# A half-precision-split transformer layer on one core: where two halves of an attention sum are joined, and how mean and variance are finished

## The chip, the cores and the metric

The kernel runs on one core of a Trainium2 chip. The metric is the time of one execution on the device in microseconds (us). The core has a matrix engine (TensorE, "PE" in the profile, its weight loads "PEld"), a vector engine (VectorE, "DVE"), an activation engine (ScalarE, "ACT"), a general engine (GpSimd, "POOL") and a queue engine that here only issues transfers (SyncE, "SP"). Each engine works through its own list of instructions in order; between engines the program orders work by semaphores.

## The reference

One pre-norm transformer layer over 8192 tokens (4 sequences of 2048) of width 256:

```python
x = x + attn(_layernorm(x), Wq, Wk, Wv, Wo)      # 16 heads of 16, causal, window 64
x = x + ffn(_layernorm(x), W1, b1, W2, b2)       # W1, W2 rounded to -1, 0, 1; relu; 1024 wide

def _layernorm(x, axis=-1, eps=1e-05):
    m = jnp.mean(x, axis=axis, keepdims=True)
    v = jnp.var(x, axis=axis, keepdims=True)
    return (x - m) / jnp.sqrt(v + eps)
```

Both norms need, for each token, the negative mean and the variance plus 1e-5. The attention output of a token is the sum over at most 64 keys of softmax weight times value.

## The kernel before

The tokens are cut into 16 chunks of 512. The whole program is written as one loop over slots n (16 slots belong to a chunk, about 2.5 us each in the steady part), and every engine walks the same slots with a list of what it does in each. Work of three chunks is in flight at a time: stage A (norm, Q, K and V of the next chunk), the attention of the present one (16 steps n, four for each group g of four heads), and stage C (output projection, second norm and feed-forward of the chunk before). The slot of each piece is fixed by the tables at the head of the file. A value is carried as a high and a low half-precision part, so many results are written twice, first by ACT (high), then by DVE (low).

In each slot n the attention goes through all engines: PE writes the scores into a PSUM bank (`scores`, L924); DVE takes the negative maximum (`negm`, L671); ACT takes the exponential and its sums (`p`, L457, four pairs of instructions); DVE takes the reciprocal of the sums (`rden`, L678); POOL multiplies (`p`, L358); DVE transposes 32 by 32 blocks (`pt`, L684); ACT (L466) or POOL (L376) makes the high part `th`, and POOL the low part `tl` (L382). On DVE the order within a slot is: `rden`, `pt`, `o_add` where there is one, `negm`, then the work of stages C and A, the statistics last.

Two places are touched by the change.

**Joining the two halves of the attention sum.** After each group g of a chunk PE has left 128 x 512 sums in the PSUM bank `pvbank` (L944): partitions 0 to 63 hold one half of each sum and 64 to 127 the other. In `o_copy` (slot 9 of the group's four) ACT copies partitions 0 to 63 into the SBUF tile `ohalf`. In `o_add` DVE adds partitions 64 to 127 to it and writes `osum`, at partitions 64 * (g % 2) on, so groups 0 and 2 go to partition 0 and groups 1 and 3 to partition 64. From the second chunk on DVE first waits until `osum` of the chunk before has been read (semaphores `s_olo0` and `s_olo1`, which POOL and DVE raise). PE's next sums wait for `s_osum`. Of a chunk's 16 slots DVE has `o_add` in slots 9 (group 0), 13 (group 1), 1 (group 2) and 5 (group 3).

**Finishing the statistics.** For stage A (`a_aggr`, once a chunk, 128 x 4 values) and stage C (`c_stats`, twice a chunk, 128 x 2 values) DVE runs its statistics instructions, then two small instructions: one writes the negative mean (`meanA`, `meanC`), the other the variance plus 1e-5 (`veA`, `veC`). Both are tensor_reduce here: the negated maximum over one element, and the sum over two, the variance and a constant 1e-5 that lies beside it in the third column of `mvA` and `mvC`. POOL then takes the power -1/2 (`rstdA`, `rstdC`) and the shift, and ACT applies them (`xnA`, `xnC`). Of a chunk's 16 slots, the two `c_stats` stand in slots 8 and 14 and `a_aggr` in slot 10.

Of the kernel before, what the change touches and what calls it, by code (L numbers as in the profile page):

```python
# [5 lines left out]
CH = 512  # L6
# [43 lines left out]
def stage_a(n, pos):  # L50
    return chunk_at(n, pos, 1)
# [4 lines left out]
def norm_at(n, pos):  # L56
    c, late = stage_a(n, pos), stage_a(n - 7, pos)
    return late if late in (1, 2) else None if c in (1, 2) else c
# [8 lines left out]
def stage_c(n, pos):  # L67
    return chunk_at(n, pos, -1)

def group_at(n, lag):
    g, r = divmod(n - lag, 4)
    return g if r == 0 and 0 <= g < 4 * NCH else None
# [3 lines left out]
def values_at(n, lag):  # L77
    return 0 if n == lag + 2 else group_at(n, lag) or None
# [34 lines left out]
def build(nc, x_d, wq_d, wk_d, wv_d, wo_d, w1_d, b1_d, w2_d, b2_d, identf_d, mask_d, maskf_d, out_d):  # L113
    f32, f16, b16 = mybir.dt.float32, mybir.dt.float16, mybir.dt.bfloat16
    ALU, ACT, AX = mybir.AluOpType, mybir.ActivationFunctionType, mybir.AxisListType
# [4 lines left out]
    with ExitStack() as ctx:  # L120
        def sb(name, shape, dt):
            return ctx.enter_context(nc.sbuf_tensor(name, shape, dt))

        def sem(name):
            return ctx.enter_context(nc.semaphore(name))
# [20 lines left out]
        xTC = [sb(f"xTC{p}", [128, 2, 256], f16) for p in "hl"]  # L146
        stA = sb("stA", [128, 4, 6], f32)
        stC = sb("stC", [128, 2, 6], f32)

        mvA = sb("mvA", [128, 4, 3], f32)  # L150
        mvC = sb("mvC", [128, 2, 3], f32)
        veA = sb("veA", [128, 4], f32)
        veC = sb("veC", [128, 2], f32)
        meanA = sb("meanA", [128, 4], f32)
        meanC = sb("meanC", [128, 2], f32)
# [15 lines left out]
        th = [sb(f"th{i}", [128, 1600], f16) for i in range(2)]  # L171
        tl = [sb(f"tl{i}", [128, 1600], f16) for i in range(2)]
        osum = sb("osum", [128, 2, CH], f32)
        ohalf = sb("ohalf", [64, CH], f32)
        oT = [sb(f"oT{p}", [128, 2, CH], f16) for p in "hl"]
        hT = [sb(f"hT{p}", [128, 8, CH // 2], f16) for p in "hl"]
        bt = sb("bt", [128, F + D], f32)
# [6 lines left out]
        sbank, pvbank, cbank = banks[0:3], banks[3], banks[6:8]  # L184
# [14 lines left out]
        s_alo, s_cdv, s_osum, s_olo1 = sem("s_alo"), sem("s_cdv"), sem("s_osum"), sem("s_olo1")  # L199
        s_stA, s_agA, s_mvA, s_xnA = sem("s_stA"), sem("s_agA"), sem("s_mvA"), sem("s_xnA")  # L200
        s_stC, s_agC, s_mvC, s_xnC = sem("s_stC"), sem("s_agC"), sem("s_mvC"), sem("s_xnC")
# [6 lines left out]
        s_oc, s_ohi, s_whi, s_abs, s_mask = sem("s_oc"), sem("s_ohi"), sem("s_whi"), sem("s_abs"), sem("s_mask")  # L208
# [3 lines left out]
        s_car, s_oh0, s_olo0, s_hp = sem("s_car"), sem("s_oh0"), sem("s_olo0"), sem("s_hp")  # L212
# [206 lines left out]
        def _(e):  # L419
# [101 lines left out]
                             a_bank(c, w)[:, :].rearrange("p (a b) -> p a b", b=64), ACT.Copy, scale=1 / WS).then_inc(s_ahi, 1)  # L521

            def o_copy(gg):
                e.wait_ge(s_pv, gg + 1)
                e.activation(ohalf[:, :], pvbank[0:64, :], ACT.Copy).then_inc(s_oc, 1)

            def c_t(c, h):
                e.wait_ge(s_c, USE[c, f"t{h}"] + 1)
# [8 lines left out]
            for n in SLOTS:  # L537
# [23 lines left out]
                c = stage_c(n, X_DMA)  # L561
# [5 lines left out]
                gg = values_at(n, PV_LAG + 1)  # L567
                if gg is not None:
                    o_copy(gg)
                for h in range(2):  # L570
                    c = stage_c(n, C_T[h] + 1)
                    if c is not None:
                        c_t(c, h)
                    for f in range(4):
                        c = stage_c(n, C_F[h] + f + 1)
                        if c is not None:
                            c_f(c, h, f)
                for t in range(2):
                    c = stage_a(n, A_T[t] + 1)
                    if c is not None:  # L580
                        a_t(c, t)
                    c = stage_a(n, A_Q[t] + 1)
                    if c is not None:
                        a_q(c, t)
                    c = stage_a(n, A_K[t] + 1)
                    if c is not None:
                        a_k(c, t)
                    c = stage_a(n, A_V[t] + 1)
# [4 lines left out]
                for u in range(2):  # L593
                    c = stage_c(n, C_NORM[u])
                    if c is not None:
                        c_norm(c, u)
                    c = norm_at(n, A_NORM[u])
                    if c is not None and (c, u) != (0, 1):
                        a_norm(c, u)
                gg = group_at(n, O_SPLIT1)  # L600
# [4 lines left out]
        def _(e):  # L605
            def consts():
                e.memset(mhalf[:, :], -0.5).then_inc(s_const, 1)
                e.memset(mvA[:, :, 2:3], 1e-5)
                e.memset(onesf[:, :], 1.0)
                e.memset(ones[:, :], 1.0).then_inc(s_const, 1)  # L610
                e.memset(mvC[:, :, 2:3], 1e-5)

# [86 lines left out]
            def a_aggr(c):  # L701
                e.wait_ge(s_stA, 4 * c + 4)
                if c >= 1:
                    e.wait_ge(s_rsA, c)
                for t in range(4):
                    ins = e.bn_aggr(mvA[:, t, 0:2], stA[:, t, :])
                ins.then_inc(s_agA, 1)
                e.wait_ge(s_agA, c + 1)
                e.tensor_reduce(meanA[:, :], mvA[:, :, 0:1], AX.X, ALU.max, negate=True)
                e.tensor_reduce(veA[:, :], mvA[:, :, 1:3], AX.X, ALU.add).then_inc(s_mvA, 1)  # L710

            def a_t(c, k):
                w = 8 * c + k
# [22 lines left out]
                                       scalar=1 / WS, in1=hi, op0=ALU.mult, op1=ALU.subtract).then_inc(s_alo, 1)  # L736

            def o_add(gg):
                c, g = gg // 4, gg % 4
                e.wait_ge(s_oc, gg + 1)  # L740
                if c >= 1:
                    e.wait_ge((s_olo0, s_olo1)[g // 2], c)
                e.tensor_tensor(osum[64 * (g % 2):64 * (g % 2) + 64, g // 2, :], pvbank[64:128, :], ohalf[:, :],
                                ALU.add).then_inc(s_osum, 1)

            def o_low(c):
                e.wait_ge(s_ohi, c + 1)
# [8 lines left out]
            def c_stats(c, u):  # L756
                h = 2 * c + u
                e.wait_ge(s_cdv, USE[c, f"wo{u}"] + 1)
                for t in range(2):
                    e.bn_stats(stC[:, t, :], xs[c % NX][:, 2 * u + t, :]).then_inc(s_stC, 1)  # L760
                e.wait_ge(s_stC, 2 * h + 2)
                if h >= 1:
                    e.wait_ge(s_rsC, h)
                for t in range(2):
                    ins = e.bn_aggr(mvC[:, t, 0:2], stC[:, t, :])
                ins.then_inc(s_agC, 1)
                e.wait_ge(s_agC, h + 1)
                e.tensor_reduce(meanC[:, :], mvC[:, :, 0:1], AX.X, ALU.max, negate=True)
                e.tensor_reduce(veC[:, :], mvC[:, :, 1:3], AX.X, ALU.add).then_inc(s_mvC, 1)

            def c_t(c, h):
                e.wait_ge(s_chi, SPLIT[c, f"t{h}"] + 1)
# [10 lines left out]
            for n in SLOTS:  # L783
                if n == SLOTS[0]:
                    consts()
# [17 lines left out]
                gg = values_at(n, O_ADD)  # L803
                if gg is not None:
                    o_add(gg)
                if 0 <= n - L_MAX < NQ:
                    biggest(n - L_MAX)
                for u in range(2):
                    c = stage_c(n, C_WO[u] + 1)
                    if c is not None:  # L810
                        residual(c, u, f"wo{u}")
                    c = stage_c(n, C_T[u] + 1)
                    if c is not None:
                        c_t(c, u)
                    for f in range(4):
                        c = stage_c(n, C_F[u] + f + 1)
                        if c is not None:
                            c_f(c, u, f)
                    c = stage_c(n, C_Y[u] + 2)
                    if c is not None:  # L820
                        residual(c, u, f"y{u}")
                for t in range(2):
                    c = stage_a(n, A_T[t] + 1)
                    if c is not None:
                        a_t(c, t)
                    c = stage_a(n, A_Q[t] + 1)
                    if c is not None:
                        a_q(c, t)
                    c = stage_a(n, A_K[t] + 1)
                    if c is not None:  # L830
                        a_k(c, t)
                    c = stage_a(n, A_V[t] + 1)
# [4 lines left out]
                for u in range(2):  # L837
                    c = norm_at(n, A_STATS[u])
                    if c is not None:
                        a_stats(c, u)  # L840
                        if u:
                            a_aggr(c)
                    c = stage_c(n, C_STATS[u])
                    if c is not None:
                        c_stats(c, u)
                gg = group_at(n, O_SPLIT1)
# [294 lines left out]
```

## Time and profile before

| | |
|---|---|
| runs | 710.91, 713.70, 713.49 us; median 713.49 us |
| the profiled execution | 710.91 us, its span 709.1 us |
| mean granted clock of TensorE, as a share of full speed | 0.986 |
| busy share of the span | PE 93%, ACT 90%, DVE 88%, POOL 84% |
| one chunk in the steady part | 40.0 us, from 98.85 us to about 618.85 us, 13 times |
| DVE busy in such a chunk | 37.1 to 37.8 us |

"Busy" counts the time in which at least one instruction of the engine runs. An instruction's start as recorded usually lies 0.07 to 0.09 us ahead of the recorded end of the one before it on DVE, since the engine takes it in while the last one drains; so what an instruction costs its engine is the distance from its start to the next start, not its own duration. The chain of work that ended last, which part 4 of the page sums up, is followed back from the last instruction: at each step to what released it. The steady part repeats itself to within a few hundredths of a us from chunk to chunk, so one chunk (338.85 to 378.85 us) stands for the others.

### The profile page before, as it was taken

What the parts mean: (1) busy time and instruction counts of PE and PEld (TensorE: products, weight loads), DVE (VectorE), ACT (ScalarE), POOL (GpSimd) and SP (SyncE); (2) the same over time, 40 slices, a digit from 0 to 9 for tenths busy, and PEclk for the clock granted to TensorE, in tenths of its full rate; (3) what the DMA queues carried; (4) which work ended last, traced back from release to release, by engine and by line L of the source; (5) the groups of instructions that cost most, each with busy time, mean ns of one, the idle gap of its engine ahead of it and who ended that gap; (6) DMA issues with size and microseconds to landing.
All of it is one profiled execution on the core that took longest, in us unless ns stands there. A gap on an engine that the chain in (4) does not pass through costs nothing.

```text
span 709.1 us, 24653 instructions
## 1 busy us (share of the span) xinstructions
PE 662.0 (93%) x8168; PEld 564.2 (80%) x8168; DVE 627.4 (88%) x1596; ACT 636.1 (90%) x2680; POOL 597.6 (84%) x836
## 2 busy tenths in 40 slices
PE   7649779999999999999999999999999999998796
PEld 4437568888888888888888888888888888887685
DVE  5697888999999899999999899999999899898764
ACT  3778989999999999999999999999999999998832
POOL 8277999898989989898989989898989989889820
PEclk9979999999999999999999999999999999999999
DMA  8575436365554636455464637465554536352000
GB/s 294 101 103 79 64 55 74 75 83 96 69 99 80 85 68 96 79 73 108 70 95 86 86 69 97 74 78 106 72 90 65 81 69 75 73 60 47 17 31 31
DMA packets 430773, 57.65 MB, mean 81 GB/s; under 512 B 403380, under 2 KB 422198, under 8 KB 430648
## 3 DMA queue, kind: packets, MB, share of 16 engines
q1 hardware_dynamic: 419784, 46.97, 44.9%
q10 hardware_dynamic: 10864, 9.11, 4.6%
q8 instruction: 66, 1.08, 0.7%
q14 instruction: 59, 0.48, 0.2%
HBM read 12.00 MB, written 8.39 MB: 29 GB/s over the span
## 4 chain that ended last, share of the span: by engine, by line
ACT 32%; PE 28%; POOL 17%; issue 14%; DVE 7%; DMA 1%; ACTq 1%; SPq 0%; POOLq 0%; DVEq 0%
ACT p L457 15%; POOL p L358 7%; PE ps L1034 6%; POOL tl L382 6%; PE ps L981 5%; ACT xnC L484 4%; PE ps L944 4%; ACT xnA L474 3%; PE ps L1007 3%; PE ps L924 3%; PE ps L992 3%; POOL th L376 2%; DVE negm L671 2%; ACT hTh L534 2%; PE ps L1046 2%
## 5 line engine op out<-in xcount | busy, mean ns | idle before, releaser
L457 ACT ACTIVATE p<-ps,negm 128x96 f32<-128x96 f32 x1024 | 341.4, 379 | 13.7 <-DVE negm L671 13.6
L382 POOL TENSOR_TENSOR tl<-pt,th 128x384 f16<-128x384 f32 x256 | 235.3, 919 | 50.6 <-ACT th L466 39.0
L457 ACT ACTIVATION_READ_ACCUMULATOR p<-ps,negm 128x1 f32 x1024 | 252.2, 247 | 0.0
L358 POOL TENSOR_TENSOR p<-p,rden 128x384 f32<-128x384 f32 x256 | 211.9, 828 | 12.9 <-DVE rden L678 11.5
L684 DVE STREAM_TRANSPOSE pt<-p 128x384 f32<-128x384 f32 x256 | 141.7, 554 | 11.5 <-POOL p L358 9.9
L671 DVE TENSOR_REDUCE negm<-ps 128x4 f32<-128x384 f32 x256 | 135.6, 530 | 6.7 <-PE ps L924 4.5
L924 PE MATMUL ps<-k,qbd 128*128 128x96 f16 x2048 | 130.0, 207 | 0.0
L924 PEld LDWEIGHTS ps<-k,qbd 128*128 128x128 f16 x2048 | 116.5, 99 | 13.5 <-issue 0.5
L944 PE MATMUL ps<-th,vb 128*128 128x96 f16 (+1 forms) x1120 | 97.9, 203 | 10.5 <-POOL tl L382 5.3
L944 PEld LDWEIGHTS ps<-th,vb 128*128 128x128 f16 x1120 | 92.6, 98 | 13.3 <-POOL tl L382 8.6
L1034 PE MATMUL ps<-xTCh,w1T 128*128 128x256 f16 x512 | 97.6, 272 | 0.0
L944 PE MATMUL ps<-tl,vb 128*128 128x96 f16 (+1 forms) x1120 | 97.3, 203 | 0.0
L944 PEld LDWEIGHTS ps<-tl,vb 128*128 128x128 f16 x1120 | 92.2, 98 | 0.0
L534 ACT ACTIVATE hTh<-ps 128x512 f16<-128x512 f32 x128 | 79.9, 624 | 13.2 <-PE ps L1034 13.0
L780 DVE SCALAR_TENSOR_TENSOR hTl<-ps,hTh 128x512 f16<-128x512 f32 x128 | 86.4, 677 | 4.7 <-ACT hTh L534 4.7
L376 POOL CAST th<-pt 128x384 f16<-128x384 f32 x144 | 72.4, 503 | 0.8 <-PE ps L944 0.8
L1034 PE MATMUL ps<-xTCl,w1L 128*128 128x256 f16 x256 | 69.8, 273 | 0.0
L1034 PE MATMUL ps<-xTCl,w1T 128*128 128x256 f16 x256 | 69.7, 272 | 0.0
L919 PE MATMUL ps<-mask,identb 128*128 128x256 bf16 x240 | 65.9, 275 | 3.1 <-ACT p L457 3.1
L466 ACT ACTIVATE th<-pt 128x384 f16<-128x384 f32 x112 | 64.3, 574 | 3.3 <-DVE pt L684 3.2
L1046 PE MATMUL ps<-w2T,hTl 128*128 128x256 f16 x512 | 66.5, 273 | 0.5 <-DVE hTl L780 0.5
L1046 PE MATMUL ps<-w2T,hTh 128*128 128x256 f16 x512 | 66.4, 273 | 0.0
(136 smaller groups left out, 1406.3 us busy)
## 6 DMA issues: line engine op xcount, KB each, us to landing
k<-kst SPq DMA_DIRECT2D x62, 288.0 KB, 4.1
vb<-vd SPq DMA_DIRECT2D x256, 32.0 KB, 2.6
out<-x SPq DMA_DIRECT2D x32, 256.0 KB, 2.4
qbd<-qs SPq DMA_DIRECT2D x252, 32.0 KB, 2.4
x<-in_L_attn_hidden ACTq DMA_DIRECT2D x15, 512.0 KB, 5.1
vb<-in_L_ffn_W SPq DMA_DIRECT2D x2, 1024.0 KB, 8.4
k<-kst ACTq DMA_DIRECT2D x2, 288.0 KB, 3.7
x<-in_L_attn_hidden SPq DMA_DIRECT2D x1, 256.0 KB, 3.2
```

The source lines that it names most:

```text
L358: e.tensor_tensor(p3, p3, rden[n % 4][:, :].unsqueeze(2).to_broadcast([128, 4, 96]), ALU.mult).then_inc(s_nm, 1)
L376: e.tensor_copy(th[g % 2][:, o], pt[n % 3][:, :]).then_inc(s_hp, 1)
L382: e.tensor_tensor(tl[g % 2][:, o], pt[n % 3][:, :], th[g % 2][:, o], ALU.subtract).then_inc(s_lo, 1)
L457: ins = e.activation(p[:, 96 * u:96 * u + 96], bank[:, 96 * u:96 * u + 96], ACT.Exp, bias=m[:, u:u + 1], accum_out=r[:, u:u + 1])
L534: e.activation(hT[0][:, 2 * f:2 * f + 2, :].rearrange("p a b -> p (a b)"), c_bank(c, f"f{h}{f}")[:, :], ACT.Relu).then_inc(s_chi, 1)
L671: e.tensor_reduce(negm[n % 4][:, :], sbank[n % 3][:, 0:384].rearrange("p (a b) -> p a b", b=96), AX.X, ALU.max, negate=True).then_inc(s_mx, 1)
L684: e.transpose(pt[n % 3][:, :], pr[n % NP][:, :]).then_inc(s_tr, 1)
L780: e.scalar_tensor_tensor(out=lo, in0=c_bank(c, f"f{h}{f}")[:, :], scalar=0.0, in1=hi, op0=ALU.max, op1=ALU.subtract).then_inc(s_cdv, 1)
L924: ins = e.matmul(bank[:, 96 * u:96 * u + 96], qbd[g // 2][:, g % 2, 128 * blk:128 * blk + 128], ks[g][:, m, 32 * blk:32 * blk + 96], start ...
L944: ins = e.matmul(pvbank[:, 32 * i0:32 * i1], lhs, rhs, start=(k == k0 and tt is th), stop=(k == 15), skip_group_check=True)
L1034: ins = e.matmul(bank[:, o], w, xTC[xp][:, k, :], start=(xp + k == 0), stop=(xp + k == 2))
L1046: ins = e.matmul(bank[:, o], hT[hp][:, f, t * 128:(t + 1) * 128], w2T[:, f, :], start=False, stop=(f == 7 and hp == 1))
```

## The change

In the statistics the two tensor_reduce of each pair become tensor_scalar, with immediate scalars: the mean times -1, the variance plus 1e-5. The constant column and its two memsets go. Nothing is moved to another place.

In the joining of the sums ACT now copies partitions 64 to 127 of `pvbank` straight into `osum`, at the partitions where the result belongs, and DVE adds partitions 0 to 63 of `pvbank` to it in place. The tile `ohalf` goes. The wait for `s_olo0` or `s_olo1` goes from DVE's `o_add` to ACT's `o_copy`.

```diff
@@ ACT
             def o_copy(gg):
+                c, g = gg // 4, gg % 4
                 e.wait_ge(s_pv, gg + 1)
-                e.activation(ohalf[:, :], pvbank[0:64, :], ACT.Copy).then_inc(s_oc, 1)
+                if c >= 1:
+                    e.wait_ge((s_olo0, s_olo1)[g // 2], c)
+                e.activation(osum[64 * (g % 2):64 * (g % 2) + 64, g // 2, :], pvbank[64:128, :],
+                             ACT.Copy).then_inc(s_oc, 1)
@@ DVE, consts
-                e.memset(mvA[:, :, 2:3], 1e-5)
...
-                e.memset(mvC[:, :, 2:3], 1e-5)
@@ DVE, a_aggr
-                    ins = e.bn_aggr(mvA[:, t, 0:2], stA[:, t, :])
+                    ins = e.bn_aggr(mvA[:, t, :], stA[:, t, :])
...
-                e.tensor_reduce(meanA[:, :], mvA[:, :, 0:1], AX.X, ALU.max, negate=True)
-                e.tensor_reduce(veA[:, :], mvA[:, :, 1:3], AX.X, ALU.add).then_inc(s_mvA, 1)
+                e.tensor_scalar(meanA[:, :], mvA[:, :, 0], -1.0, None, ALU.mult)
+                e.tensor_scalar(veA[:, :], mvA[:, :, 1], 1e-5, None, ALU.add).then_inc(s_mvA, 1)
@@ DVE, o_add
-                c, g = gg // 4, gg % 4
+                g = gg % 4
+                dst = osum[64 * (g % 2):64 * (g % 2) + 64, g // 2, :]
                 e.wait_ge(s_oc, gg + 1)
-                if c >= 1:
-                    e.wait_ge((s_olo0, s_olo1)[g // 2], c)
-                e.tensor_tensor(osum[64 * (g % 2):64 * (g % 2) + 64, g // 2, :], pvbank[64:128, :], ohalf[:, :],
-                                ALU.add).then_inc(s_osum, 1)
+                e.tensor_tensor(dst, pvbank[0:64, :], dst, ALU.add).then_inc(s_osum, 1)
@@ DVE, c_stats
-                e.tensor_reduce(meanC[:, :], mvC[:, :, 0:1], AX.X, ALU.max, negate=True)
-                e.tensor_reduce(veC[:, :], mvC[:, :, 1:3], AX.X, ALU.add).then_inc(s_mvC, 1)
+                e.tensor_scalar(meanC[:, :], mvC[:, :, 0], -1.0, None, ALU.mult)
+                e.tensor_scalar(veC[:, :], mvC[:, :, 1], 1e-5, None, ALU.add).then_inc(s_mvC, 1)
```

DVE's list at the end of slot 8 and the start of slot 9 of a chunk, before: the pair of the statistics, what stands right behind it, and the first `o_add` of the chunk. The names ahead of the arrow are what is written, those behind it what is read (`ps` is a PSUM bank).

```order
L765 BN_AGGR mvC<-stC 128x2 [waits s_rsC,s_stC]
L765 BN_AGGR mvC<-stC 128x2
L768 TENSOR_REDUCE meanC<-mvC 128x2 [waits s_agC]
L769 TENSOR_REDUCE veC<-mvC 128x2
L678 RECIPROCAL rden<-rsum 128x4 [waits s_nm,s_ex]
L684 STREAM_TRANSPOSE pt<-p 128x384 [waits s_lo,s_nm]
L743 TENSOR_TENSOR osum<-ps,ohalf 64x512 [waits s_olo0,s_oc]
L671 TENSOR_REDUCE negm<-ps 128x4 [waits s_ex,s_sc]
```

The same place in the changed kernel:

```order
L763 BN_AGGR mvC<-stC 128x2 [waits s_rsC,s_stC]
L763 BN_AGGR mvC<-stC 128x2
L766 TENSOR_SCALAR meanC<-mvC 128x2 [waits s_agC]
L767 TENSOR_SCALAR veC<-mvC 128x2
L678 RECIPROCAL rden<-rsum 128x4 [waits s_nm,s_ex]
L684 STREAM_TRANSPOSE pt<-p 128x384 [waits s_lo,s_nm]
L742 TENSOR_TENSOR osum<-ps,osum 64x512 [waits s_oc]
L671 TENSOR_REDUCE negm<-ps 128x4 [waits s_ex,s_sc]
```

Every instruction stands where it stood; two have another operation, and `o_add` has one wait less and reads its own output tile.

## Rows read from the trace of the kernel before

**Rows 1.** The page: busy time and share; shares of the chain that ended last.
```profile
PE 662.0 (93%) x8168; PEld 564.2 (80%) x8168; DVE 627.4 (88%) x1596; ACT 636.1 (90%) x2680; POOL 597.6 (84%) x836
...
ACT 32%; PE 28%; POOL 17%; issue 14%; DVE 7%; DMA 1%; ACTq 1%; SPq 0%; POOLq 0%; DVEq 0%
```

**Rows 2.** Windows: length, busy PE, PEld, DVE, ACT, POOL, clock, DMA share, GB/s.
```profile
338.85:378.85 40.00, 39.77 (x505) 34.24 (x504) 37.61 (x98) 38.76 (x167) 36.15 (x52) 1.00 0.55 85
```

**Rows 3.** The chain in order of time, one chunk: start, time on the chain, what.
```profile
373.72 0.04 DVE meanC L768
...
373.79 0.06 DVE veC L769
...
375.25 0.57 DVE negm L671
...
377.12 1.10 ACT xnC L484 x2
...
378.26 0.66 PE ps L1019 x4
```

**Rows 4.** Timeline, slot 8 into 9: start, duration, engine, line, operation, [idle before].
```profile
373.07 0.91 POOL L382 TENSOR_TENSOR tl<-pt,th 128x384 f16<-128x384 f32 x1
...
373.72 0.15 DVE L768 TENSOR_REDUCE meanC<-mvC 128x2 f32<-128x2 f32 x1
...
373.94 0.55 DVE L684 STREAM_TRANSPOSE pt<-p 128x384 f32<-128x384 f32 x1
374.11 0.83 POOL L358 TENSOR_TENSOR p<-p,rden 128x384 f32<-128x384 f32 x1
...
374.52 0.69 DVE L743 TENSOR_TENSOR osum<-ps,ohalf 64x512 f32<-64x512 f32 x1
...
375.25 0.56 DVE L671 TENSOR_REDUCE negm<-ps 128x4 f32<-128x384 f32 x1
...
375.72 0.74 DVE L699 BATCH_NORM_STATS2 stA<-x 128x6 f32<-128x256 f32 x2
...
375.84 0.34 ACT L457 ACTIVATE p<-ps,negm 128x96 f32<-128x96 f32 x1 [0.75 <-DVE negm L671]
```

**Rows 5.** Timeline near 39 us, in the weights' preparation: DVE and POOL.
```profile
39.08 0.92 POOL L382 TENSOR_TENSOR tl<-pt,th 128x384 f16<-128x384 f32 x1
...
39.24 0.78 DVE L648 TENSOR_SCALAR nthr<-thr 128x2 f32<-128x2 f32 x1
...
39.96 0.83 POOL L358 TENSOR_TENSOR p<-p,rden 128x384 f32<-128x384 f32 x1
```

**Rows 6.** Timeline near 644 us: a DVE operation that reads two SBUF tiles.
```profile
643.91 0.92 POOL L382 TENSOR_TENSOR tl<-pt,th 128x384 f16<-128x384 f32 x1
...
644.79 1.28 POOL L358 TENSOR_TENSOR p<-p,rden 128x384 f32<-128x384 f32 x1
...
644.16 1.22 DVE L748 TENSOR_TENSOR oTl<-osum,oTh 128x512 f16<-128x512 f32 x1
```

**Rows 7.** Timeline, slot 14: the second pair of stage C and what follows.
```profile
347.60 0.51 POOL L376 CAST th<-pt 128x384 f16<-128x384 f32 x1
...
348.08 0.15 DVE L768 TENSOR_REDUCE meanC<-mvC 128x2 f32<-128x2 f32 x1
...
348.19 0.91 POOL L382 TENSOR_TENSOR tl<-pt,th 128x384 f16<-128x384 f32 x1
...
350.40 0.33 ACT L457 ACTIVATE p<-ps,negm 128x96 f32<-128x96 f32 x1
```

**Rows 8.** Timeline, slot 10: the pair of stage A.
```profile
378.55 0.16 DVE L709 TENSOR_REDUCE meanA<-mvA 128x4 f32<-128x4 f32 x1
...
378.70 0.91 POOL L382 TENSOR_TENSOR tl<-pt,th 128x384 f16<-128x384 f32 x1 [1.19 <-ACT th L466]
```

**Rows 9.** Timeline of ACT, slot 5: the copy of a group's sums and its follower.
```profile
362.93 0.66 ACT L525 ACTIVATE ohalf<-ps 64x512 f32<-64x512 f32 x1
363.40 0.67 ACT L534 ACTIVATE hTh<-ps 128x512 f16<-128x512 f32 x1
```

More of the change, by code:

```diff
@@ L148, in build @@
         stC = sb("stC", [128, 2, 6], f32)
-        mvA = sb("mvA", [128, 4, 3], f32)
-        mvC = sb("mvC", [128, 2, 3], f32)
+        mvA = sb("mvA", [128, 4, 2], f32)
+        mvC = sb("mvC", [128, 2, 2], f32)
         veA = sb("veA", [128, 4], f32)
@@ L173, in build @@
         osum = sb("osum", [128, 2, CH], f32)
-        ohalf = sb("ohalf", [64, CH], f32)
         oT = [sb(f"oT{p}", [128, 2, CH], f16) for p in "hl"]
@@ L764, in c_stats @@
                 for t in range(2):
-                    ins = e.bn_aggr(mvC[:, t, 0:2], stC[:, t, :])
+                    ins = e.bn_aggr(mvC[:, t, :], stC[:, t, :])
                 ins.then_inc(s_agC, 1)
                 e.wait_ge(s_agC, h + 1)
-                e.tensor_reduce(meanC[:, :], mvC[:, :, 0:1], AX.X, ALU.max, negate=True)
-                e.tensor_reduce(veC[:, :], mvC[:, :, 1:3], AX.X, ALU.add).then_inc(s_mvC, 1)
+                e.tensor_scalar(meanC[:, :], mvC[:, :, 0], -1.0, None, ALU.mult)
+                e.tensor_scalar(veC[:, :], mvC[:, :, 1], 1e-5, None, ALU.add).then_inc(s_mvC, 1)
             def c_t(c, h):
```

## The prediction

> **What bounds the kernel now.** I read the page first [rows 1]: four engines are busy 84 to 93% of the span, and the chain that ended last runs over ACT, PE and POOL, with only 7% on DVE. DVE's busy total thus says little; what matters is the places where DVE stands on that chain. The windows show a steady part of 13 chunks of 40.0 us; in one, PE is busy 39.8 us, ACT 38.8, DVE 37.6 and POOL 36.2 [rows 2]. Nothing in it has more than some 4 us to spare, and a delay of a few tenths at the wrong place is seen in every chunk. So I followed the chain through one chunk [rows 3]. It goes over DVE from 371 to 375.8 us, through `meanC`, `veC`, the transpose, `o_add` and `negm`; then ACT, which has been idle for 0.75 us waiting for that very `negm` [rows 4], and `xnC`, for which PE waits. That is slot 8 into 9: one of the three pairs and one of the four `o_add` of a chunk lie on the chain there, one right behind the other. At the other places the chain is on PE (slots 10 to 15) and then on ACT and POOL, and DVE has slack.
>
> The Trainium skill, SBUF — State Buffer, section "Who interferes with whom", has this as a rule that speaks against the change: tensor_scalar in SBUF may take the port pair that DVE shares with GpSimd, for a whole instruction, tensor_reduce never does. The trace agrees, with 0.78 us against 0.15 us.
>
> Now each pair by its place. **Slot 8**, on the chain: in all 13 chunks the pair starts with 0.22 to 0.27 us of a `tl` left (here 373.72 against 373.98). The first tensor_scalar ends at 374.00 instead of 373.87, the second 0.07 behind it as now. POOL's next operation needs `rden`, which stands behind the pair, so it can't come between. Cost +0.13 us (0.09 in three chunks), 13 times: +1.6 us. If the release cost the full 0.15 us of an instruction instead of 0.02, it would be +0.26 us each, +3.4 us. **Slot 10**: POOL is idle when the pair starts and for another 0.15 us [rows 8]; the pair has 0.07 us between its starts, so both are in first. Cost 0; the `tl` behind may be pushed by 0.05 us. **Slot 14**: the pair starts 0.03 us ahead of the end of a POOL cast, and a `tl` starts 0.11 us after the pair's start [rows 7], in 11 chunks alike. Whether the second tensor_scalar gets in ahead of that `tl` is a toss-up. If it loses, the pair ends with the `tl` at 349.12, and DVE is 0.8 to 0.9 us late. Then `negm` ends near 350.2 instead of 349.3, and ACT takes it up at 350.40 [rows 7]: 0.2 us of slack are left. The other takers (POOL's `p` 0.25 us late, the transposes, the low parts) have more, and DVE makes up the rest in its idle times before slot 5. I take 0.05 us a chunk, +0.6 us, with ends of 0 and 0.3 us (+3.9 us). The few pairs before 130 us and behind 618 us meet 0 to 0.25 us of a POOL operation: +0.4 us. At the very end, where two pairs stand on the chain, POOL is idle: nothing. The two memsets are ahead of a wait for the first transfer: nothing.
>
> **The join.** Both instructions keep size and duration (0.69 us on DVE, 0.6 on ACT). The waits that move to ACT are for work of the chunk before, over four slots (10 us) old: they never hold, on DVE now or on ACT then; nothing queued behind them waits. DVE waits for ACT's copy as before; at slot 9 the copy is long done. What changes is the partitions. DVE usually starts an instruction 0.08 us ahead of the end of the one before, as `stA` behind `negm` (375.72 against 375.81), but `o_add` starts 0.03 us after the end of the transpose and `negm` 0.04 us after the end of `o_add` [rows 4]. It is so at all 64 of them, and also for groups 0 and 2, whose output lies at partition 0; there the only operand that doesn't start at partition 0 is the PSUM half at 64. The change removes it: for groups 0 and 2 everything starts at partition 0. I expect both gaps gone: 0.11 us ahead of `o_add`, 0.12 us behind it, and 0.04 us in `negm`, which takes 0.56 us there and 0.52 elsewhere. At slot 9 (group 0) that is -0.27 us on the chain, 13 times: -3.5 us. At slot 1 (group 2) DVE has slack: nothing. Groups 1 and 3 still start at 64, now for the SBUF input as well: gaps stay, possibly with a third on the instruction behind `negm` (+0.12 us on DVE, off the chain, but it brings the slot 14 pair nearer to the `tl`).
>
> The Trainium skill, VectorE: DVE Perf Modes, section "Two Vector instructions with no wait between them", has a model: an instruction is held until the one before ends if an operand starts in another quadrant than the last of its kind. Gaps of 0.03 and 0.04 us in the trace agree; by the model the even groups lose two holds and the odd ones get a third. No run so far shows the even case without the offset.
>
> On ACT the copy's source now starts at partition 64 in all four groups. No ACT instruction of the trace starts elsewhere than at 0, so I bound it: below by nothing, above by what DVE shows, the loss of the overlap on both sides. ACT's overlap at the copy is 0.66 - 0.47 = 0.19 us [rows 9], so up to 0.3 to 0.4 us a copy, of which those of slots 1 and 5 stand on the chain. I take nothing, as DVE's gap at the even groups is the only sign of such a thing, and on another engine.
>
> **The sum**, against the profiled execution (span 709.1, 710.9 us in all): +1.6 + 0.6 + 0.4 - 3.5 = -0.9 us, 710.0 us. The median of the runs shown is 713.5, 0.36% above that execution; I scale: 712.6 us. Less than 0.5% (3.6 us) can't be told from no change here.
>
> **The rivals.** (1) The gaps at `o_add` stay, for instance since they belong to an operation on 64 partitions. Then the sum is +2.6 us: 716.1 us. For it: I have no row without the offset. Against: instructions of 2 to 512 elements overlap alike elsewhere, so the shape alone is no likely cause. (2) The pairs cost what they can: slower. The place is slot 14: the tensor_scalar loses to the `tl`, and `negm` comes later than ACT's 350.40. It decides at a DVE delay of about 1.0 us; I expect 0.9, so it takes little (a full 0.15 us behind the release, and 0.1 us from the third gap). With 0.3 us there and 0.26 us at slot 8: -0.9 + 1.8 + 3.3 = +4.2 us with the gain at `o_add`, 717.7 us, and up to 721 us without it. For it: the chunk fits to a few hundredths, and POOL's idle time before that `tl` is only 0.08 us. Against: the slack of 0.2 us and the order of starts. (3) ACT is held like DVE by the start at 64: two copies a chunk at 0.3 us on the chain, 13 chunks, +7.8 us, 720.4 us with the rest. Against: no sign of it. (4) Faster by more than the bound: `o_add` gains its 3.5 us and the pairs slip in between POOL's operations once phases move, so that they cost under 0.5 us, and a part of slot 1's 0.27 us counts as well: -4 us, 709.5 us or less.
>
> **How the numbers follow.** The forecast has 0.42. Rival 1 has 0.22, rival 2 has 0.20, rival 3 has 0.08, rival 4 has 0.08. The forecast and rival 1 are within 0.5%: 0.64. Rivals 2 and 3 are slower: 0.28. Faster: 0.08. The range runs from 709.0 (rival 4, and the lower half of the runs' spread) to 719.5 us, which takes in most of rival 2 and leaves rival 3 out.
>
> **What the profile after would show.** Tensor_scalar `meanC` at slot 8 of 0.28 us against 0.15, ended within 0.03 us of a `tl`; at slot 14 either 0.15 or near 1 us. `o_add` of groups 0 and 2 starting 0.08 us ahead of the transpose's end, groups 1 and 3 not. The steady chunk at 39.8 to 40.0 us. ACT's distance from the copy to its follower 0.48 us as now. The prediction is wrong if that distance grows, if ACT's idle time before the `p` of slot 15 grows from nothing, or if the pairs at slot 10 stall.

## The result, and the profile after

The changed kernel takes 718.2 us (median of 4 runs, 717.0 to 719.0) against 713.6 us for the kernel before in the same comparison: ratio 1.0073, 95% interval 1.0044 to 1.0101. It is slower, by less than 1%, where no change that can be told was forecast. Its profiled execution took 717.62 us, with a span of 715.8 us, 6.7 us longer than before. The medians lie only 4.6 us apart, since the profiled execution of the kernel before is the shortest of its runs (710.91 us; the other three take 713.5 to 713.7 us). The mean granted clock is nearly the same (0.983 against 0.986).

The page's busy times and shares of the chain, to be read against [rows 1]:

```profile
PE 669.0 (93%) x8168; PEld 563.8 (79%) x8168; DVE 633.6 (89%) x1594; ACT 650.8 (91%) x2680; POOL 598.8 (84%) x836
...
PE 37%; ACT 29%; POOL 15%; issue 11%; DVE 5%; DMA 1%; ACTq 1%; SPq 0%; POOLq 0%; DVEq 0%
```

ACT has as many instructions as before and shows 14.7 us more busy time; DVE has two fewer (the memsets) and shows 6.2 us more. One steady chunk (window; length, busy PE, PEld, DVE, ACT, POOL, clock) answers to [rows 2]:

```profile
338.90:379.38 40.48, 40.08 (x507) 34.25 (x506) 38.21 (x98) 39.79 (x168) 36.34 (x52) 1.00 0.52 83
```

The chunk is 40.5 us long instead of 40.0. As the median distance from one slot 8 to the next over ten steady chunks it is 40.49 us against 39.99, and thirteen such chunks make 6.5 of the 6.7 us; the mean of the ten differs by 0.48 us, which makes 6.2. So the question is what lengthens a chunk by 0.5 us.

Slot 8 into 9, timeline of DVE and of POOL in the changed kernel (start, duration, engine, line, operation), as [rows 4]:

```profile
376.71 0.29 DVE L766 TENSOR_SCALAR meanC<-mvC 128x2 f32<-128x2 f32 x1
376.92 0.15 DVE L767 TENSOR_SCALAR veC<-mvC 128x2 f32<-128x2 f32 x1
376.98 0.17 DVE L678 RECIPROCAL rden<-rsum 128x4 f32<-128x4 f32 x1
377.07 0.54 DVE L684 STREAM_TRANSPOSE pt<-p 128x384 f32<-128x384 f32 x1
377.54 0.64 DVE L742 TENSOR_TENSOR osum<-ps,osum 64x512 f32<-64x512 f32 x1
378.12 0.53 DVE L671 TENSOR_REDUCE negm<-ps 128x4 f32<-128x384 f32 x1
378.58 0.72 DVE L699 BATCH_NORM_STATS2 stA<-x 128x6 f32<-128x256 f32 x2
```
```profile
376.06 0.91 POOL L380 TENSOR_TENSOR tl<-pt,th 128x384 f16<-128x384 f32 x1
377.23 0.83 POOL L356 TENSOR_TENSOR p<-p,rden 128x384 f32<-128x384 f32 x1 [0.25 <-DVE rden L678]
```

This is the place that the prediction was worked out for, and it came out as written, to 0.02 us: `meanC` takes 0.29 us and ends at 377.00, 0.03 us after the `tl`; `o_add` of group 0 starts 0.07 us ahead of the transpose's end, `negm` 0.06 us ahead of the end of `o_add`. From the transpose's start to the end of `negm` it is 1.58 us, against 1.87 us in [rows 4].

Slot 14, as [rows 7]: DVE, POOL, and ACT's `p` that waits for the `negm` of this stretch.

```profile
350.63 0.93 DVE L766 TENSOR_SCALAR meanC<-mvC 128x2 f32<-128x2 f32 x1
351.48 0.15 DVE L767 TENSOR_SCALAR veC<-mvC 128x2 f32<-128x2 f32 x1
...
352.11 0.51 DVE L671 TENSOR_REDUCE negm<-ps 128x4 f32<-128x384 f32 x1
```
```profile
350.62 0.91 POOL L380 TENSOR_TENSOR tl<-pt,th 128x384 f16<-128x384 f32 x1
```
```profile
352.34 0.60 ACT L511 ACTIVATE kst<-ps 128x512 f16<-128x512 f32 x1 [0.25 <-PE ps L979]
352.83 0.33 ACT L455 ACTIVATE p<-ps,negm 128x96 f32<-128x96 f32 x1
```

Here it is the first tensor_scalar that loses to the `tl`, not the second, and waits it out: 0.93 us, in ten chunks alike. `negm` still ends at 352.62, 0.21 us ahead of ACT's `p`.

What is new is on ACT. Its copies in slots 1 (group 2) and 5 (group 3), timeline of ACT, as [rows 9]. First the kernel before, slot 1 and the instruction ahead of the copy in slot 5:

```profile
351.66 1.10 ACT L484 ACTIVATE xnC<-x,shiftC,rstdC 128x255 f32<-128x255 f32 x2
352.64 0.59 ACT L525 ACTIVATE ohalf<-ps 64x512 f32<-64x512 f32 x1
353.12 0.59 ACT L534 ACTIVATE hTh<-ps 128x512 f16<-128x512 f32 x1
...
361.94 1.17 ACT L474 ACTIVATE xnA<-x,shiftA,rstdA 128x256 f32<-128x256 f32 x2
```

The changed kernel:

```profile
354.09 1.11 ACT L482 ACTIVATE xnC<-x,shiftC,rstdC 128x255 f32<-128x255 f32 x2
355.22 0.59 ACT L526 ACTIVATE osum<-ps 64x512 f32<-64x512 f32 x1
355.84 0.60 ACT L536 ACTIVATE hTh<-ps 128x512 f16<-128x512 f32 x1
```
```profile
364.68 1.21 ACT L472 ACTIVATE xnA<-x,shiftA,rstdA 128x256 f32<-128x256 f32 x2
365.92 0.59 ACT L526 ACTIVATE osum<-ps 64x512 f32<-64x512 f32 x1
366.53 0.60 ACT L536 ACTIVATE hTh<-ps 128x512 f16<-128x512 f32 x1
```

Each copy starts 0.02 to 0.03 us after the instruction before it has ended, and the next one 0.02 to 0.03 us after the copy; in [rows 9] the follower starts 0.19 us ahead of the copy's end. The distance from copy to follower is 0.61 to 0.62 us instead of 0.47 to 0.48, and ahead of the copy 0.15 us (slot 1) and 0.25 us (slot 5) are lost as well: from `xnC` to the copy it is 1.13 us against 0.98, from `xnA` 1.24 us against 0.99. And the copy is on the chain, in order of time, at both places:

```profile
355.22 0.59 ACT osum L526
...
365.92 0.59 ACT osum L526
```

### The profile page after: what moved, and what is told of

It reads as the page before. It is cut to its first block, busy times and chain, and to the rows that moved or that the text cites. A ratio compares the mean times of both kernels' runs of the same rounds, so it can differ in the third digit from the quotient of the medians.

```text
span 715.8 us, 24651 instructions
## 1 busy us (share of the span) xinstructions
PE 669.0 (93%) x8168; PEld 563.8 (79%) x8168; DVE 633.6 (89%) x1594; ACT 650.8 (91%) x2680; POOL 598.8 (84%) x836
## 4 chain that ended last, share of the span: by engine, by line
PE 37%; ACT 29%; POOL 15%; issue 11%; DVE 5%; DMA 1%; ACTq 1%; SPq 0%; POOLq 0%; DVEq 0%
ACT p L455 15%; PE ps L1044 6%; PE ps L1032 6%; POOL tl L380 6%; PE ps L942 5%; POOL p L356 5%; PE ps L979 5%; PE ps L990 4%; PE ps L922 4%; ACT xnA L472 3%; PE ps L1005 3%; ACT xnC L482 2%; POOL th L374 2%; ACT osum L526 2%; ACT xTAh L495 2%
## 5 line engine op out<-in xcount | busy, mean ns | idle before, releaser
L455 ACT ACTIVATION_READ_ACCUMULATOR p<-ps,negm 128x1 f32 x1024 | 249.5, 244 | 0.0
L464 ACT ACTIVATE th<-pt 128x384 f16<-128x384 f32 x112 | 62.8, 560 | 2.9 <-DVE pt L684 2.8
```

What stands on the lines that cost most here:

```text
L455: ins = e.activation(p[:, 96 * u:96 * u + 96], bank[:, 96 * u:96 * u + 96], ACT.Exp, bias=m[:, u:u + 1], accum_out=r[:, u:u + 1])
```

## The experiments

Theory J says: an ACT instruction that starts at another partition than its neighbours loses its overlap on both sides, two of a chunk's four copies stand on the chain, and that is the loss. Theory S says: the stall in slot 14's pair is. "Chunk" below is the median distance between slots 8 over ten steady chunks of the profiled execution, from about 173 us on. In five of the profiled executions (join_only, copy_low_half, the two of the pairs, add_after_max) one of the ten chunks is 0.2 to 0.7 us longer than the one that answers to it four chunks later; the median hardly moves by it.

| kernel | chunk, us | ratio to before, 95% interval |
|---|---|---|
| before | 39.99 | |
| changed | 40.49 | 1.0073 (1.0044 to 1.0101) |
| join_only | 40.36 | 1.0041 (1.0023 to 1.0058) |
| stats_only | 40.09 | 1.0018 (1.0002 to 1.0033) |
| join_g0 | 39.70 | 0.9958 (0.9943 to 0.9973) |
| join_g1 | 39.98 | 1.0010 (0.9995 to 1.0025) |
| join_g2 | 40.26 | 1.0040 (1.0025 to 1.0054) |
| join_g3 | 40.29 | 1.0047 (1.0031 to 1.0063) |
| copy_low_half | 40.28 | 1.0051 (1.0031 to 1.0071) |
| slot14_reduce | 40.50 | 1.0083 (1.0059 to 1.0108) |
| slot8_reduce | 40.40 | 1.0040 (1.0027 to 1.0053) |
| add_after_max | 39.74 | 0.9924 (0.9907 to 0.9940) |
| add_after_max_g0 | 39.74 | 0.9929 (0.9914 to 0.9943) |

The chunk comes from one profiled execution of each kernel and tells of the steady part alone; the ratio is that of the medians of the whole. The two do not always go together: 13 times 0.37 us are 4.8 us for join_only, its ratio makes 2.9 us (1.6 to 4.1). The kernel before ran from 709.5 to 714.3 us in that comparison, and its profiled execution (710.9 us) is one of its short ones.

**The two parts apart.** join_only has the changed `o_copy` and `o_add` in the kernel before; stats_only has the changed statistics alone.

> Only the join of the sums is changed, the statistics stay tensor_reduce. Theory J (ACT's copy out of partition 64 is held on both sides, two of a chunk's four copies stand on the chain): the copy keeps its 0.62 us to the next ACT instruction against 0.48, a steady chunk of 40.3 to 40.5 us, 4 to 6 us in all, ratio 1.006 to 1.009. Theory S (the stall of 0.9 us in the pair of slot 14 makes the chunk longer): 39.7 us a chunk from the gain at o_add, -3.5 us, ratio 0.995.

> Only the statistics are changed to tensor_scalar, the join stays as before. Theory J: meanC at slot 8 takes 0.28 us and costs 0.13 us a chunk on the chain, slot 14 is covered whether it stalls or not: chunk 40.1 us, +1.5 us, ratio 1.001 to 1.003. Theory S: slot 14 stalls by 0.8 to 0.9 us as it does with both changes, and the chunk is 40.4 to 40.7 us, ratio 1.006 to 1.01.

The join alone makes the chunk 0.37 us longer (40.36), the statistics alone 0.10 us (40.09); together they give 40.46 of the measured 40.49. So three quarters of the loss belong to the join, though its DVE part gains. This is theory J. The chunk of join_only came as expected (40.3 to 40.5 us); its ratio did not, 1.0041 with an interval that ends at 1.0058, where 1.006 to 1.009 was expected. In stats_only the pair of slot 14 doesn't even stall (DVE, then POOL):

```profile
349.39 0.17 DVE L765 TENSOR_SCALAR meanC<-mvC 128x2 f32<-128x2 f32 x1
```
```profile
348.90 0.51 POOL L375 CAST th<-pt 128x384 f16<-128x384 f32 x1
349.49 0.92 POOL L381 TENSOR_TENSOR tl<-pt,th 128x384 f16<-128x384 f32 x1
```

It starts 0.10 us ahead of the `tl` and is through, the second one too; in the changed kernel it starts 0.01 us behind it. A tenth of a us decides between 0.17 and 0.93 us. The expectation for stats_only had a range of 1.001 to 1.003 in time and held; that slot 14 stalls was left open in it.

**Which copies cost.** Four kernels have the new join for one group only:

```diff
 def o_copy(gg):
-    e.activation(ohalf[:, :], pvbank[0:64, :], ACT.Copy).then_inc(s_oc, 1)
+    if g == G:          # 0, 1, 2 or 3
+        ...             # wait for s_olo0 or s_olo1, copy pvbank[64:128] into osum
+    else:
+        e.activation(ohalf[:, :], pvbank[0:64, :], ACT.Copy).then_inc(s_oc, 1)
 def o_add(gg):
+    if g == G:
+        e.tensor_tensor(dst, pvbank[0:64, :], dst, ALU.add).then_inc(s_osum, 1)
+        return
...
```

> The new join for group 0 of each chunk alone (slot 9); groups 1 to 3 and the statistics as before. Under both theories DVE gains 0.11 + 0.12 + 0.04 us on the chain there. Theory J: the hold on ACT's copy falls into the 0.75 us in which ACT waits for negm anyway and costs nothing: chunk 39.7 us, -3.5 us, ratio 0.995. If ACT's hold at slot 9 does reach the chain: 40.0 to 40.1 us, ratio 1.000 to 1.002.

> The new join for group 2 alone (slot 1), all else as before. ACT's copy there stands on the chain, and DVE's gain of 0.27 us does not. With the hold on both sides of ACT's copy (0.15 us ahead of it, 0.14 behind it): chunk 40.3 us, ratio 1.004 to 1.006. If the chain goes another way there: 40.0 us.

> The new join for group 3 alone (slot 5), all else as before. The copy stands on the chain as well: 0.25 us ahead of it and 0.14 behind it, chunk 40.3 to 40.4 us, ratio 1.004 to 1.007. Groups 0, 2 and 3 together must give the 40.37 us of the kernel with the join alone: -0.28 + 0.29 + 0.36. If the chain goes another way there: 40.0 us.

> The new join for group 1 alone (slot 13), all else as before. PE sets the chain there, so ACT's hold (0.2 + 0.14 us) and DVE's third hold should be covered: chunk 40.0 us, ratio 0.999 to 1.002. The single joins so far add up to -0.28 + 0.25 + 0.30 = +0.27 us a chunk, the join of all four costs 0.37; if group 1 isn't covered, it costs the 0.1 us that is missing, chunk 40.1 us.

Group 0 alone gains 0.29 us a chunk, groups 2 and 3 alone lose 0.27 and 0.30 us, group 1 nothing. In join_g0 the copy loses its overlap as well (ACT, slot 9): it starts after the instruction ahead of it has ended, and the `p` behind it 0.62 us later.

```profile
369.91 0.65 ACT L466 ACTIVATE th<-pt 128x384 f16<-128x384 f32 x1
370.58 0.59 ACT L529 ACTIVATE osum<-ps 64x512 f32<-64x512 f32 x1
371.20 0.34 ACT L457 ACTIVATE p<-ps,negm 128x96 f32<-128x96 f32 x1
...
373.11 0.34 ACT L457 ACTIVATE p<-ps,negm 128x96 f32<-128x96 f32 x1
```

But there ACT had 0.75 us to wait for `negm` [rows 4]. That cover takes the loss; the last row, the `p` of the next step, has no idle time recorded ahead of it any more. DVE's gain stays and the kernel is 0.4% faster than before. In join_g1 the same loss is covered too: the chain there is on PE.

The sum of the four single joins is +0.27 us (-0.29 - 0.01 + 0.27 + 0.30), the join of all four +0.37. The missing 0.1 us is not in group 1, and is left open: with several copies changed the chain need not take the same way between them. That it takes another is seen in join_only, whose chain goes from POOL's `tl` straight to PE at the place where that of the kernel before goes over DVE [rows 3]:

```profile
372.89 0.93 POOL tl L382
...
373.86 1.46 PE ps L946 x32
```

What length this gives or takes was not measured.

**What on ACT causes it.** copy_low_half has the join as changed and the statistics as before, but ACT copies partitions 0 to 63 and DVE adds 64 to 127:

```diff
-    e.activation(osum[...], pvbank[64:128, :], ACT.Copy).then_inc(s_oc, 1)
+    e.activation(osum[...], pvbank[0:64, :], ACT.Copy).then_inc(s_oc, 1)
-    e.tensor_tensor(dst, pvbank[0:64, :], dst, ALU.add).then_inc(s_osum, 1)
+    e.tensor_tensor(dst, pvbank[64:128, :], dst, ALU.add).then_inc(s_osum, 1)
```

> The join as changed (copy into osum, add in place), but ACT copies partitions 0 to 63 and DVE adds 64 to 127; statistics as before. Two readings of theory J: if only the source's start counts on ACT, all four copies have 0.48 us to the next instruction and the chunk is as before, 40.0 us, ratio 1.000. If the output's start counts as well, groups 1 and 3, whose output lies at partition 64, have 0.6 us and groups 0 and 2 have 0.48: one such copy stands on the chain (slot 5), chunk 40.2 to 40.3 us, ratio 1.003 to 1.006. DVE keeps its gaps at all four o_add, since its PSUM input starts at 64.

ACT's timeline in it, group 1 (output at partition 64) and group 2 (everything at partition 0):

```profile
344.48 0.41 ACT L457 ACTIVATE p<-ps,negm 128x96 f32<-128x96 f32 x1
344.70 0.28 ACT L457 ACTIVATION_READ_ACCUMULATOR p<-ps,negm 128x1 f32 x1
345.00 0.59 ACT L528 ACTIVATE osum<-ps 64x512 f32<-64x512 f32 x1
345.62 0.34 ACT L457 ACTIVATE p<-ps,negm 128x96 f32<-128x96 f32 x1
...
354.07 1.10 ACT L484 ACTIVATE xnC<-x,shiftC,rstdC 128x255 f32<-128x255 f32 x2
355.05 0.59 ACT L528 ACTIVATE osum<-ps 64x512 f32<-64x512 f32 x1
355.52 0.59 ACT L538 ACTIVATE hTh<-ps 128x512 f16<-128x512 f32 x1
```

Group 1's copy starts 0.02 us after the end of the accumulator read ahead of it, and its follower is 0.62 us behind; group 2's is 0.47 us behind. So an output at partition 64 alone is enough; and from join_g2, where output is at 0 and only the source at 64, a source alone is enough too (354.03 to 354.65):

```profile
352.90 1.10 ACT L484 ACTIVATE xnC<-x,shiftC,rstdC 128x255 f32<-128x255 f32 x2
354.03 0.60 ACT L529 ACTIVATE osum<-ps 64x512 f32<-64x512 f32 x1
354.65 0.60 ACT L541 ACTIVATE hTh<-ps 128x512 f16<-128x512 f32 x1
```

The copies of groups 0 and 2 in copy_low_half have the same added wait for `s_olo0` or `s_olo1` as those of the changed kernel and keep their overlap, so the wait that was moved to ACT costs nothing. This kernel's chunk is 40.28 us, as the second reading said, with one such copy on the chain (slot 5) and no gain on DVE.

**The pairs by place.** In the changed kernel, one of stage C's two pairs goes back to tensor_reduce, and the constant column that it needs comes back with it:

```diff
+                if u == 1:      # slot14_reduce; u == 0 for slot8_reduce
+                    e.tensor_reduce(meanC[:, :], mvC[:, :, 0:1], AX.X, ALU.max, negate=True)
+                    e.tensor_reduce(veC[:, :], mvC[:, :, 1:3], AX.X, ALU.add).then_inc(s_mvC, 1)
+                else:
+                    ...         # tensor_scalar as in the changed kernel
```

> The changed kernel with the pair of slot 14 back as tensor_reduce; the pairs of slots 8 and 10 stay tensor_scalar. If the stall of 0.93 us there costs time: the chunk is shorter than the changed kernel's 40.48 us by 0.1 us and more. If it is covered, as the two single changes say by adding up (40.37 + 0.11): 40.48 us, the same as the changed kernel, ratio to before 1.007.

> The changed kernel with the pair of slot 8 back as tensor_reduce, the pairs of slots 14 and 10 as changed. The 0.13 us by which the first tensor_scalar waits for a tl stands on the chain there: chunk 40.37 us, 0.11 us less than the changed kernel, ratio to before 1.005. If the cost is not at slot 8: 40.48 us.

slot14_reduce has no stall in slot 14 any more, its `negm` now ends 0.98 us ahead of the `p` (DVE, then ACT), and the chunk is 40.50 us, the same as with the stall:

```profile
352.06 0.16 DVE L768 TENSOR_REDUCE meanC<-mvC 128x2 f32<-128x2 f32 x1
...
352.75 0.52 DVE L672 TENSOR_REDUCE negm<-ps 128x4 f32<-128x384 f32 x1
```
```profile
354.25 0.33 ACT L455 ACTIVATE p<-ps,negm 128x96 f32<-128x96 f32 x1
```

So 0.77 us of stall in every chunk costs nothing: theory S has fallen. slot8_reduce takes 0.09 us off the chunk (40.40), which is the wait of 0.13 us at slot 8, or most of it. In it the pair of slot 14, still tensor_scalar, mostly takes 0.17 us.

**The stretch at slot 9 itself.** The gain in join_g0 suggests taking `o_add` off that stretch altogether. add_after_max is the kernel before with group 0's `o_add` behind `negm`; add_after_max_g0 has the new join for group 0 besides.

```diff
-                if gg is not None:
+                if gg is not None and gg % 4:
                     o_add(gg)
                 if 0 <= n - L_MAX < NQ:
                     biggest(n - L_MAX)
+                if gg is not None and gg % 4 == 0:
+                    o_add(gg)
```

> The kernel before with one change: in slot 9 o_add of group 0 stands behind negm instead of ahead of it. Takes the whole of o_add off the place where ACT waits 0.75 us for negm. If this stretch of the chain is what I take it for, the chunk loses 0.6 to 0.75 us (39.3 to 39.4 us), ratio 0.988 to 0.991; if another wait is right behind it, as little as 0.2 us, 0.996.

> The same order together with the new join for group 0. With o_add off the chain the DVE gain of the new join counts no more, and ACT's hold at slot 9 (0.26 + 0.14 us) is no longer covered by an idle time: 0 to 0.3 us a chunk longer than with the order alone, ratio 0.990 to 0.997.

Both are faster than before, at 0.9924 and 0.9929, the fastest kernels here; their intervals overlap. But the chunk is 39.74 us, not 39.3 to 39.4, and no shorter than join_g0's 39.70. My expectation was right on the sign and wrong on the size of the gain in the chunk. The shares of the chain by line in join_g0, from 338 to 378 us and from 378 to 418 us:

```profile
by line: PE ps L1043 17.5%; PE ps L1055 17.5%; PE ps L953 14.2%; PE ps L933 14.0%; PE ps L990 12.9%; PE ps L1016 6.6%; PE ps L1001 6.5%; PE ps L928 3.3%; PE ps L1028 2.6%; PE ps L979 2.2%; PE ps L925 1.6%; PE ps L1050 1.1%; issue 0.0%
```
```profile
by line: ACT p L457 18.7%; PE ps L1055 8.7%; PE ps L953 8.2%; PE ps L1001 6.5%; PE ps L1043 6.5%; PE ps L990 6.5%; PE ps L933 6.1%; issue 5.8%; ACT hTh L540 3.6%; ACT xnA L474 3.4%; PE ps L1016 3.3%; POOL tl L382 3.3%; ACT ohalf L531 2.9%;
```

In the first stretch there is nothing but PE on it, and in add_after_max likewise. But that is the rarer case: of the ten stretches of 40 us from 178 us on it is so in three of join_g0 and in two of add_after_max; in the others ACT and POOL stand on the chain as well, ACT's `p` with 18 or 19% of it. The 0.75 us of waiting at slot 9 is thus not what the chunk can lose: three kernels that free the slot in different ways all stop at 39.70 to 39.74 us. PE is busy for 119.7 of the 120 us from 340 to 460 us in join_g0 (119.3 in the kernel before), so it is the likely next bound, with 0.1 us a chunk left; that it is the bound is not shown. The 0.3% by which the reordered kernels beat join_g0 in time does not come from the steady chunks. Between the profiled executions of join_g0 and add_after_max_g0 it is 1.9 us: 0.8 ahead of the first slot 8, 0.4 up to the second, 0.6 between the last two.

## Why the prediction was wrong

**The step that failed** is the copy on ACT: "I take nothing, as DVE's gap at the even groups is the only sign of such a thing, and on another engine". The bound beside it, 0.3 to 0.4 us a copy with those of slots 1 and 5 on the chain, was the right term. Measured are 0.15 + 0.14 us at slot 1 and 0.25 + 0.14 us at slot 5, and 0.27 and 0.30 us of chunk length when each is changed alone. Rival 3 was thus what happened, and it was given a chance of 0.08. Its price, 7.8 us over 13 chunks, compares with 7.4 us from the two single joins; with the rest of the sum it is +6.9 us on the profiled execution, where 6.7 were measured. The mistake was one of weighing: for an unknown with two ends I took the end at nothing, though the nearest row (the same 64 to 127 of the same bank, read by DVE) lay at the other end. I had even used that row to credit the change with a gain. That the measured 718.2 us lies inside the stated range, and within 0.5 us of rival 2's 717.7, is luck: the range was stretched for a loss in the pairs that did not happen, and rival 3's 720.4 us was left out of it.

The scaling was a smaller error, and one that hid part of the first: 0.36% was put on top because the median of the kernel before lay that far above its profiled execution; for the changed kernel the two lie 0.08% apart. On the profiled executions the forecast is 7.6 us too low (710.0 against 717.6), on the medians 5.6. For the same reason rival 3's 720.4 us lie 2.2 us above the measured median, though its sum fits the profiled execution.

**The gain at `o_add`**, -0.27 us a chunk, was right: 1.58 us from transpose to the end of `negm` against 1.87. Some 0.05 us of it is that the addition itself is recorded with 0.64 us instead of 0.69, where the prediction had it keep its duration. join_g0 has -0.29 us in the chunk. Rival 1, that the gaps stay, is refuted. The odd groups keep both gaps and get a third: the instruction behind `negm` starts 0.03 us after its end in the changed kernel (slot 5, timeline of DVE), against 0.08 us ahead of it before.

```profile
367.26 0.56 DVE L671 TENSOR_REDUCE negm<-ps 128x4 f32<-128x384 f32 x1
367.85 0.69 DVE L778 SCALAR_TENSOR_TENSOR hTl<-ps,hTh 128x512 f16<-128x512 f32 x1
```

The model of the Trainium skill (VectorE: DVE Perf Modes, section "Two Vector instructions with no wait between them") holds an instruction when an operand starts in another quadrant (a group of 32 partitions) than the last of its kind. The trace agrees with it in all three cases: two holds before, none in the even groups and three in the odd ones after. That page speaks of the Vector engine; here ACT shows the like.

One reading of the prediction was too wide: `o_add` starts 0.03 us after the transpose's end at 47 of the 64 places before, and not at every one. At none does it start ahead of it, so the argument holds. But in slot 5 it starts 0.38 us after it, since DVE waits there for ACT's copy (0.53 us in the changed kernel):

```profile
363.62 0.69 DVE L743 TENSOR_TENSOR osum<-ps,ohalf 64x512 f32<-64x512 f32 x1 [0.38 <-ACT ohalf L525]
```

**The pair of slot 8**: `meanC` of 0.28 us was forecast and 0.29 measured, +0.13 us; the chunk shows 0.09 to 0.13 us of it. With 0.10 us in stats_only the 13 chunks make 1.3 us, against 1.6 in the sum.

**The pair of slot 14**: the toss-up fell to the stall, but on the first tensor_scalar. "0.2 us of slack are left" was right (0.21 us), and the stall costs nothing, not 0.05 us. Rival 2 put the loss here, and slot14_reduce refutes it. **Slot 10** met no `tl`, as forecast.

**The waits moved to ACT** cost nothing, as forecast.

Put together, with measured sizes: 13 x (-0.29 + 0.27 + 0.30 + 0.10) = +4.9 us, and with the 0.1 us a chunk that only the join of all four shows, +6.2 us of the 6.7 us by which the span grew. The forecast sum had the terms -3.5 and +1.6, besides +0.6 for slot 14, which cost nothing, and +0.4 for the pairs outside the steady part, which no run shows apart, and lacked +7.4.

## What to carry to other kernels

A gain from moving an operand's start partition on one engine can be a loss on the engine that takes over the offset: price both sides with the same row, and give the change only to those places where the side that loses has to wait anyway. Here the join costs 0.4% in all four groups and gains 0.4% in group 0 alone. A stall of 0.8 us that is seen in every chunk can be worth nothing, and 0.15 us that hardly shows in a busy time can be the whole loss; only where the chain passes counts, and an experiment with one place changed at a time shows it. Before work on such a place, see how far the next bound is: here an engine waited 0.75 us at the place, and no kernel got more than 0.3 us a chunk out of it.

## What the runs showed of the hardware

- ACT: a copy whose source or whose output starts at partition 64, among instructions at partition 0, starts 0.02 to 0.03 us after the one before has ended, and its follower 0.02 to 0.03 us after it; with everything at partition 0 the follower starts 0.47 to 0.48 us after the copy's start instead of 0.61 to 0.62 us. Either side's offset is enough, and a further semaphore wait doesn't do it.
- DVE: a small tensor_scalar in SBUF that came 0.01 us after the start of a POOL operation waited for all of it (0.93 us); one that came 0.10 us ahead took 0.17 us.
- DVE: with nothing offset the 64x512 addition is recorded with 0.64 us instead of 0.69, on top of the overlap that it gets back (changed kernel, groups 0 and 2; groups 1 and 3 have 0.68).
